# Last phase of a two-layer kernel: input norm statistics moved to ScalarE, and one scale and reciprocal for both hidden tiles

## The chip, the cores and the metric

The kernel runs on one core of one Trainium2 chip. The time is that of the device in microseconds (us) for one execution. An execution was profiled by itself; its time stands beside its span, from the first to the last instruction. The engines are TensorE (PE; PEld is its weight load), VectorE (DVE), ScalarE (ACT), GpSimd (POOL) and SyncE (SP), which issues direct transfers. They run side by side, each through its own list of instructions in order, and wait for one another on semaphores.

## The reference

Two layers work on x of shape 16 x 256 x 128 in float32. Each has a token-mixing part and a feed-forward part, and each part adds to x what it computes from a layer norm of x:

```
x = x + L0_attn(layernorm(x))     # gated linear attention
x = x + L0_ffn(layernorm(x))      # shared expert and one of 8 routed experts
x = x + L1_attn(layernorm(x))     # input projection, conv of 4 taps, state scan, gate, output projection
x = x + L1_ffn(layernorm(x))      # FP4-quantised gate, up and down projection
layernorm(x) = (x - mean(x)) / sqrt(var(x) + 1e-5)    # over the last 128 values
```

L1_attn takes 256 inner values: `xs = silu(conv(x w_in))`, a scan `h = 0.9 h + 0.1 (xs w_B)`, and `y = (h w_C) * silu(z)`, projected by `w_out`. L1_ffn quantises its input and its hidden vector in blocks of 16: `scale = max(|block|) / 6`, at least 1e-12; each value over its scale goes to the nearest point of an FP4 grid and is multiplied by the scale again. The hidden vector has 352 values, 22 blocks.

## The kernel before

Three phases follow one another: attention and shared expert of layer 0 (`phase_ab`), the routed experts (`phase_c`), and the whole of layer 1 (`phase_d`), which is the only one that the change touches. `phase_d` starts at 372 us and fills the rest of the span.

A token lies on one of the 128 partitions, so the 256 tokens of a sequence are a pair of tiles of 128 x 128. `phase_d` is a software pipeline over the 16 sequences. Each engine runs `body(j)` for j from -4 to 15; `run_skewed` writes out -4 to 0 and 11 to 15, and puts 1 to 10 in a hardware loop, two to a pass, in which semaphore values and tile addresses come from registers. POOL's list is written out in full. Within one body five sequences are worked on at different stages: `e = j + 4` has its input norm, `a = j + 3` its projection, convolution (on PE, as shifted products), Silu and scan, `b = j + 2` the gate, the output projection, the second norm and the input quantiser, `c = j + 1` the gate and up products and the hidden quantiser, and `d = j` the rescale, the down product and the store.

The order within a body is written by hand, and every hand-off is a semaphore. An engine that waits holds back all that stands behind.

- The input norm of e: DVE runs two bn_stats (`norm_stats`, L1835) early in the body and two bn_aggr (`norm_aggr`, L1842) later, which give mean and variance of both tiles in `mv`. POOL makes the factor and the offset in four small operations (`norm_sums`, L1691 to L1698) behind those of the second norm, and then issues the two gathers that add the routed experts' rows to x for the sequence two bodies on (L1676). ACT applies the norm at the end of the body (`xn`, L1800). PE transposes `xn` in the next body (L2016).
- The second norm of b has the same form (`stats4`, `mv4`, `shift4`, `xn4`, L1771).
- ACT's order: copies of `xqT` and `xnT`, the two Silus of the feed-forward (L1758), copies of `hqT`, `xn4` of b, `xs` of a (L1778), the hidden quantiser's two magnitudes (L1302), `zs` of a (L1788), the input quantiser's magnitude, `us` (L1795), `xn` of e.
- PE's order: `ps_Y` of b from the scan (L2002), transposes of `xq` and `xn`, the output projection from `yz` (L2023), gate and up products of c, transposes of `hq`, convolution products into `ps_A` and gate products into `ps_Z` (L206 to L208), the state matmuls from `xs` (L2076), the down product (L2089).
- The hidden quantiser of c (`Fp4`, `hidden_step`) on DVE, for two tiles t: block maxima (step 0, L1314), scale (1, L1316), reciprocal (2, L1318), division (3, L1320), and two rounding steps (4 and 5, L1323 and L1324), the last in the next body; then POOL multiplies by the scale (L1298). Steps 0 to 3 are issued step by step, tile 0 and then tile 1, so that scale and reciprocal are four operations on 128 x 22.

At the start of the phase the last groups of the shared expert still run (`late_up`, `late_silu`, `late_hidden`, `late_down`) and stand ahead of, or between, the first bodies on PE, ACT and DVE.

Of the kernel before, what the change touches and what calls it, by code (L numbers as in the profile page):

```python
# [28 lines left out]
P = 128  # L29
# [1249 lines left out]
class Fp4:  # L1279
# [296 lines left out]
def phase_d(nc, io, g, out):  # L1576
# [6 lines left out]
    with ExitStack() as ctx:  # L1583
# [13 lines left out]
        stats = sb("stats", [P, 2, 6])  # L1597
        mv = sb("mv", [P, 2, 2])
# [23 lines left out]
        fp4_h = [Fp4(nc, sb, f"fh{t}", F) for t in range(2)]  # L1622
# [6 lines left out]
        def halved(a):  # L1629
# [3 lines left out]
        (s_st, s_ln, s_eps, s_pow, s_nb, s_xn, s_xp, s_xT, s_p, s_z, s_zs, s_silu, s_u, s_us, s_scan, s_yp, s_yz, s_o,  # L1633
         s_x4) = (sem(n) for n in (
             "s_st", "s_ln", "s_eps", "s_pow", "s_nb", "s_xn", "s_xp", "s_xT", "s_p", "s_z", "s_zs", "s_silu", "s_u",
             "s_us", "s_scan", "s_yp", "s_yz", "s_o", "s_x4"))
        (s_st4, s_ln4, s_eps4, s_pow4, s_nb4, s_xn4, s_qz, s_mag, s_low, s_lowq, s_qx, s_magx, s_xq, s_xqp, s_xqT, s_gu, s_sg, s_h, s_qh, s_hq, s_hp, s_hT,
         s_f, s_x5, s_out) = (sem(n) for n in (
             "s_st4", "s_ln4", "s_eps4", "s_pow4", "s_nb4", "s_xn4", "s_qz", "s_mag", "s_low", "s_lowq", "s_qx", "s_magx", "s_xq", "s_xqp", "s_xqT", "s_gu", "s_sg",
# [31 lines left out]
        @blk_.gpsimd  # L1671
        def _(pool):
            def gather(n):

                for t in (2 * n, 2 * n + 1):
                    nc.gpsimd.indirect_dma_start(  # L1676
                        out=x[:, t, :], out_offset=None, in_=g["yg_dram"][:, :],
                        in_offset=bass.IndirectOffsetOnAxis(ap=g["pos"][:, t:t + 1], axis=0),
                        compute_op=ALU.add).then_inc(s_gather[n % 2], 16)

            nc.gpsimd.memset(hs[:, :], 0.0).then_inc(s_wz, 1)
            nc.gpsimd.memset(decay[:, :], 0.9).then_inc(s_wz, 1)
# [4 lines left out]
            def norm_sums(mean_var, to, nb, s_l, s_x, s_e, s_p, s_done, j):  # L1687
                wait(pool, s_l, j)
                wait(pool, s_x, j, ago=1)
                apart(pool)  # L1690
                nc.gpsimd.tensor_scalar(to, mean_var[:, :, 1], 1.0, EPS_LN, ALU.mult, ALU.add).then_inc(s_e, 1)  # L1691
                wait(pool, s_e, j)
                nc.gpsimd.tensor_tensor(to, to, halves[:, 0:2], ALU.pow).then_inc(s_p, 1)
                wait(pool, s_p, j, per=2)
                nc.gpsimd.tensor_tensor(nb, mean_var[:, :, 0], to, ALU.mult).then_inc(s_p, 1)
                wait(pool, s_p, j, n=2, per=2)
                apart(pool)
                nc.gpsimd.tensor_scalar(nb, nb, -1.0, None, ALU.mult).then_inc(s_done, 1)  # L1698

            def body(j):  # L1700
                b, d, e = j + 2, j, j + 4
                if live(d):
                    for t in range(2):
                        wait(pool, s_qh, d, n=t + 1, per=2)
                        wait(pool, s_hp, d, n=t + 1, per=2, ago=1)
                        fp4_h[t].rescale(nc.gpsimd, hq[:, t, :]).then_inc(s_hq, 1)
                if live(b):
                    norm_sums(mv4[:, :, :], rstd4[:, :], shift4[:, :], s_ln4, s_xn4, s_eps4, s_pow4, s_nb4, b)
                if live(e):
                    norm_sums(mv[:, :, :], rstd[:, :], shift[:, :], s_ln, s_xn, s_eps, s_pow, s_nb, e)  # L1710
                if live(e + 2):
                    if (e.off + 2) % 2 == 0 and e.off + 2 >= 2 * EARLY:
                        pool.wait_ge(s_ladd, (e.off + 2 - 2 * EARLY) // 2 + 1)
                    gather(e.off + 2)

            for j in range(FIRST, LAST + 1):
                body(Seq(j))

        @blk_.scalar
        def _(act):  # L1720
# [20 lines left out]

            def body(j):
# [24 lines left out]
                if live(b):  # L1767
                    wait(act, s_nb4, b)
# [11 lines left out]
                if live(c):  # L1780
                    for t in range(2):
                        act.wait_ge(s_qz, c.lin(10, 7 + t))
                        wait(act, s_qh, c, n=t + 1, per=2, ago=1)
                        fp4_h[t].magnitude().then_inc(s_mag, 1)
# [11 lines left out]
                if live(e):  # L1796
                    wait(act, s_nb, e)
                    wait(act, s_xp, e, ago=1)
                    for t in range(2):
# [9 lines left out]
        def _(dve):  # L1809
# [19 lines left out]
            PER = 10  # L1829
# [15 lines left out]
            def hidden_step(c, n, t):  # L1845

                if n == 0:
                    wait(dve, s_h, c, n=t + 1, per=2)
                elif n == 4:
                    wait(dve, s_mag, c, n=t + 1, per=2)  # L1850
                else:
                    if n == 1:
                        wait(dve, s_hq, c, n=t + 1, per=2, ago=1)
                    dve.wait_ge(s_qz, c.lin(PER, 2 * n - 1 + t))
                fp4_h[t].step(n, hid[:, t, :]).then_inc(s_qz if n < 5 else s_qh, 1)

# [15 lines left out]
            def body(j):  # L1872
# [36 lines left out]
                if live(c):  # L1909
                    for t in range(2):  # L1910
                        wait(dve, s_sg, c, n=t + 1, per=2)
                        nc.vector.tensor_tensor(hid[:, t, :], silu[:, t, :], (ps_U, ps_Z)[t][:, 0:F], ALU.mult).then_inc(s_h, 1)
                        if t == 0 and live(b):
                            wait(dve, s_nb4, b, ago=1)
                            norm_aggr(b, stats4, mv4, s_st4, s_ln4)
                    for n in range(4):
                        for t in range(2):
                            hidden_step(c, n, t)
                elif live(b):
                    wait(dve, s_nb4, b, ago=1)  # L1920
# [199 lines left out]
```

## Time and profile before

| | |
|---|---|
| time, median of 3 runs | 615.96 us (612.94 to 616.2) |
| the profiled execution's own time | 608.28 us |
| its span, instructions | 606.5 us, 15160 |
| TensorE's mean granted clock | 0.973 |
| busy over the span: PE, PEld | 541.1 us (89%), 443.1 us (73%) |
| busy over the span: DVE, ACT, POOL | 447.7 us (74%), 316.7 us (52%), 342.8 us (57%) |
| gathers into x on POOL (L1676), 32 | 57.3 us, 1791 ns each |
| rescale on POOL (L1298), 32 | 27.9 us, 890 ns each |

"Busy" adds up the durations of an engine's instructions; waits and semaphore work are not in it. Instructions of one engine may overlap by some 0.1 us, the next starting while the last one ends, so what an instruction costs in a row is the distance from its start to the next one's. A matmul's end is modelled. A granted clock of 1.00 is TensorE's 2.4 GHz, 0.50 its 1.2 GHz.

### The profile page before, as it was taken

How to read it: one execution, taken by the hardware profiler on the slowest of the kernel's cores; microseconds unless marked ns; L12 is line 12 of the kernel's file. 1: busy time of each engine (PE TensorE's matmuls, PEld its weight loads, DVE VectorE, ACT ScalarE, POOL GpSimd, SP SyncE). 2: the span in 40 equal slices, each digit the busy share in tenths (PEclk: the TensorE clock that was granted, in tenths of full speed). 3: DMA queues.
4: the chain of work that ended last, by engine and by line, in shares of the span. 5: the costliest groups of instructions: out<-in, count | busy, mean ns of one | idle time of the engine just before them, and what ended most of it. 6: DMA issues, size and time to landing. Idle time of an engine off the chain costs nothing. (4 is left out here: it accounts for less than half of the span.)

```text
span 606.5 us, 15160 instructions
## 1 busy us (share of the span) xinstructions
PE 541.1 (89%) x4517; PEld 443.1 (73%) x4518; DVE 447.7 (74%) x1179; ACT 316.7 (52%) x899; POOL 342.8 (57%) x514
## 2 busy tenths in 40 slices
PE   1799999999999898987999997998999999999955
PEld 1557667767767577777989996787778877887854
DVE  2689999899988449933575342468999989999873
ACT  2355676666666554304655652435545565456432
POOL 5468777777777522256764103746757777673231
PEclk9999999999999999996999998999999999999976
DMA  7000100100110164015222301200111111110000
GB/s 211 22 19 29 46 28 27 49 28 26 39 39 26 56 185 119 1 33 137 68 51 56 52 27 30 28 10 9 23 32 18 17 17 22 30 17 9 10 19 17
DMA packets 35193, 25.55 MB, mean 42 GB/s; under 512 B 4752, under 2 KB 31568, under 8 KB 35152
## 3 DMA queue, kind: packets, MB, share of 16 engines
q1 hardware_dynamic: 29264, 20.32, 11.4%
q0 software_dynamic: 5888, 4.72, 5.0%
q8 instruction: 20, 0.33, 0.2%
q14 instruction: 21, 0.17, 0.1%
HBM read 14.09 MB, written 6.75 MB: 34 GB/s over the span
## 5 line engine op out<-in xcount | busy, mean ns | idle before, releaser
L1135 PE MATMUL a_ps_a<-a_qx,a_kt 32*128 32x512 f32 x512 | 69.1, 628 | 1.0 <-DMA a_qx<-a_qs 1.0
L1676 POOL DMA_INDIRECT x<-yg_dram,pos x32 | 57.3, 1791 | 10.8 <-issue 10.8
L1298 POOL TENSOR_TENSOR d_hq<-d_fh_v,d_fh_scale 128x352 f32<-128x352 f32 x32 | 27.9, 890 | 57.1 <-DVE d_fh_v L1324 57.1
L440 POOL TENSOR_SCALAR_AFFINE_SELECT a_at<-a_at 128x512 f32<-128x512 f32 x80 | 50.7, 653 | 14.4 <-ACT a_at L521 14.4
L198 POOL DMA_INDIRECT rows<-xn_dram,slot_token x40 | 40.0, 999 | 32.0 <-ACT c_rows L1447 19.0
L521 ACT ACTIVATE a_at<-a_ps_a 128x512 f32<-128x512 f32 x80 | 44.5, 599 | 11.5 <-PE a_ps_a L1135 9.9
L1490 DVE TENSOR_TENSOR c_hid<-c_act,c_ps 128x352 f32<-128x352 f32 x39 | 20.2, 519 | 38.5 <-ACT c_act L1433 38.5
L1135 PEld LDWEIGHTS a_ps_a<-a_qx,a_kt 32*128 32x128 f32 x512 | 31.7, 188 | 16.9 <-issue 16.3
L206 PE MATMUL d_ps_A<-d_xnT,wmix 128*128 128x256 f32 x128 | 37.1, 290 | 0.6 <-ACT d_silu L1758 0.6
L704 DVE TENSOR_TENSOR a_at<-a_ps_a,mask 128x512 f32<-128x512 f32 x48 | 32.8, 685 | 6.3 <-PE a_ps_a L1135 5.2
L1433 ACT ACTIVATE c_act<-c_ps 128x352 f32<-128x352 f32 x39 | 18.1, 465 | 36.7 <-PE c_ps L208 36.7
L207 PE MATMUL d_ps_A<-d_xnT,wmix 128*128 128x256 f32 x128 | 36.1, 282 | 0.0
L208 PE MATMUL d_ps_A<-d_xnT,wmix 128*128 128x256 f32 x128 | 36.0, 282 | 0.0
L1059 PE MATMUL a_ps_o<-a_at,a_vpad 128*32 128x128 f32 x1024 | 34.6, 276 | 0.0
L466 POOL TENSOR_TENSOR a_kt<-a_e,a_rope 128x512 f32<-128x512 f32 x16 | 20.4, 1277 | 21.5 <-ACT a_e L557 21.5
L1546 PE MATMUL c_ps_y<-w,c_hidT 128*128 (+1 forms) x234 | 30.0, 277 | 1.6 <-ACT c_hidT L1459 1.6
L206 PE MATMUL c_ps<-w13p,c_xT 128*128 x78 | 29.8, 382 | 1.5 <-issue 0.5
L2089 PEld LDWEIGHTS d_ps_G<-d_wd,d_hqT 128*128 128x128 f32 (+1 forms) x192 | 23.8, 199 | 8.7 <-issue 5.5
L1546 PEld LDWEIGHTS c_ps_y<-w,c_hidT 128*128 128x128 f32 (+1 forms) x234 | 27.6, 191 | 2.3 <-issue 2.2
L789 DVE RECIPROCAL a_c<-a_c 128x128 f32<-128x128 f32 x32 | 29.1, 939 | 0.0
L2089 PE MATMUL d_ps_G<-d_wd,d_hqT 128*128 128x128 f32 (+1 forms) x192 | 27.0, 292 | 2.0 <-ACT d_hqT L1766 2.0
L1059 PEld LDWEIGHTS a_ps_o<-a_at,a_vpad 128*32 128x32 f32 x1024 | 26.0, 109 | 3.4 <-issue 3.0
(336 smaller groups left out, 1758.6 us busy)
## 6 DMA issues: line engine op xcount, KB each, us to landing
a_qx<-a_qs SPq DMA_DIRECT2D x64, 64.0 KB, 1.9
a_at<-in_L_ffn_w_eDF_dram SPq DMA_DIRECT2D x16, 176.0 KB, 3.2
yg_dram<-c_y SPq DMA_DIRECT2D x19, 128.0 KB, 1.8
xn_dram<-a_xn2s SPq DMA_DIRECT2D x16, 128.0 KB, 1.9
out_dram<-x SPq DMA_DIRECT2D x16, 128.0 KB, 1.9
w<-in_L_ffn_w_eFD_dram SPq DMA_DIRECT2D x2, 512.0 KB, 5.1
x<-in_L_attn_x_dram SPq DMA_DIRECT2D x1, 768.0 KB, 5.4
rows<-xn_dram,slot_token POOLq DMA_INDIRECT x40, 2.7
```

Of the source, the lines that this page charges most:

```text
L198: nc.gpsimd.indirect_dma_start(out=g["rows"][:, k % 4, t, :], out_offset=None, in_=g["xn2_dram"][:, :], in_offset=bass.IndirectOffsetOnAxi ...
L206: nc.tensor.matmul(to, left(0), right(0), start=start, stop=False)
L207: nc.tensor.matmul(to, left(0), right(1), start=False, stop=False)
L208: return nc.tensor.matmul(to, left(1), right(0), start=False, stop=stop)
L440: nc.gpsimd.affine_select(at[:, t, r, :, :], at[:, t, r, :, :], pattern=[[0, 4], [1, P]], compare_op=ALU.is_ge, fill=0.0, base=0, channel_ ...
L521: nc.scalar.activation(at[:, t, r, :, :], ps_a[:, r, :, :], ACT.Copy).then_inc(s_copied, 1)
L704: nc.vector.tensor_tensor(at[:, t, r, :, :], ps_a[:, r, :, :], mask[:, 0:1, :].to_broadcast([P, 4, P]), ALU.mult).then_inc(s_masked, 1)
L1059: last = nc.tensor.matmul(ps_o[32 * r:32 * r + 32, tile(t)], vpad[:, b.par, t, c0:c0 + 32], at[:, t, r, h, :], start=(t == 0 and h == 0), ...
L1135: last = nc.tensor.matmul(ps_a[:, r, :, :], kt[rows, b.par, c_, tile(t)], qx[rows, b.par, :, c_, tile(t)], start=(c_ == 0), stop=(c_ == 1))
L1546: last = nc.tensor.matmul(ps_y[:, t, :], hidT[0:fn, f.par, t, n, :], w2[0:fn, e_out[t], n, :], start=(n == 0), stop=(n == 2))
L1676: nc.gpsimd.indirect_dma_start(out=x[:, t, :], out_offset=None, in_=g["yg_dram"][:, :], in_offset=bass.IndirectOffsetOnAxis(ap=g["pos"][:, ...
L2089: last = nc.tensor.matmul(ps_G[:, P * t:P * t + P], hqT[0:fn, t, f, :], wd[0:fn, f, :], start=(f == 0), stop=(f == 2))
```

## The change

The four DVE instructions of the input norm go. In their place ACT makes two passes over each tile of e: `sums`, a Copy that also adds up the row (`total`), placed ahead of the Silus; and, after POOL has made `less` = -total / 128, `squares`, a Square with bias `less` that adds up the squared deviations (`square`), placed between `xn4` of b and `xs` of a. What the two passes write elementwise goes to a tile that nobody reads. POOL makes `less` right after its rescale of the hidden tiles and, behind the second norm's operations, factor and offset from `square`: three operations where there were four. `rstd` and `shift` mean what they meant.

The hidden quantisers of the two tiles share one tensor each for maxima, scales and reciprocals. Maxima and division stay one instruction for each tile; scale and reciprocal become one instruction each on 128 x 44 (`hidden_scales`), which waits for the maxima of both tiles. Semaphores for the two norms are counted in one (`s_nb`, `s_nb4`) instead of three; that changes no order.

```diff
@@ class Fp4
-    def __init__(self, nc, sb, name, width):
+    def __init__(self, nc, sb, name, width, small=None):
-        self.amax, self.scale, self.inv = (sb(f"{name}_{n}", [P, self.blocks]) for n in ("amax", "scale", "inv"))
+        self.amax, self.scale, self.inv = small or [sb(f"{name}_{n}", [P, self.blocks]) for n in ("amax", "scale", "inv")]
@@ phase_d, gpsimd, body
                         fp4_h[t].rescale(nc.gpsimd, hq[:, t, :]).then_inc(s_hq, 1)
+                if live(e):
+                    wait(pool, s_st, e)
+                    wait(pool, s_ln, e, ago=1)
+                    apart(pool)
+                    nc.gpsimd.tensor_scalar(less[:, :], total[:, :], -1.0 / D, None, ALU.mult).then_inc(s_nb, 1)
                 if live(b):
...
                 if live(e):
-                    norm_sums(mv[:, :, :], rstd[:, :], shift[:, :], s_ln, s_xn, s_eps, s_pow, s_nb, e)
+                    wait(pool, s_ln, e)
+                    wait(pool, s_xn, e, ago=1)
+                    apart(pool)
+                    nc.gpsimd.tensor_scalar(rstd[:, :], square[:, :], 1.0 / D, EPS_LN, ALU.mult, ALU.add).then_inc(s_nb, 1)
+                    wait(pool, s_nb, e, n=2, per=4)
+                    nc.gpsimd.tensor_tensor(rstd[:, :], rstd[:, :], halves[:, 0:2], ALU.pow).then_inc(s_nb, 1)
+                    wait(pool, s_nb, e, n=3, per=4)
+                    nc.gpsimd.tensor_tensor(shift[:, :], less[:, :], rstd[:, :], ALU.mult).then_inc(s_nb, 1)
@@ phase_d, scalar
+            def sums(e):
+                act.wait_ge(s_gather[e.par], e.half(32, 32))
+                wait(act, s_nb, e, n=1, per=4, ago=1)
+                apart(act)
+                for t in range(2):
+                    last = nc.scalar.activation(unused[:, 0, t, :], x[:, e.lin(2, t), :], ACT.Copy, accum_out=total[:, t:t + 1])
+                last.then_inc(s_st, 1)
+
+            def squares(e):
+                wait(act, s_nb, e, n=1, per=4)
+                wait(act, s_nb, e, n=2, per=4, ago=1)
+                apart(act)
+                for t in range(2):
+                    last = nc.scalar.activation(unused[:, 1, t, :], x[:, e.lin(2, t), :], ACT.Square, bias=less[:, t:t + 1],
+                                                accum_out=square[:, t:t + 1])
+                last.then_inc(s_ln, 1)
...
                     late_silu(4)
+                if live(e):
+                    sums(e)
                 if live(c):
...
                     last.then_inc(s_xn4, 1)
+                if live(e):
+                    squares(e)
                 if live(a):
@@ phase_d, vector
-            PER = 10
+            PER = 8
+            amax, scale, inv = (a[:, :, :].rearrange("p t b -> p (t b)") for a in both)
...
+            def hidden_scales(c):
+
+                wait(dve, s_hq, c, n=2, per=2, ago=1)
+                dve.wait_ge(s_qz, c.lin(PER, 2))
+                nc.vector.tensor_scalar(scale, amax, -1.0 / 6.0, -1e-12, ALU.mult, ALU.min).then_inc(s_qz, 1)
+                dve.wait_ge(s_qz, c.lin(PER, 3))
+                nc.vector.reciprocal(inv, scale).then_inc(s_qz, 1)
...
-                if live(e):
-                    dve.wait_ge(s_gather[e.par], e.half(32, 32))
-                    norm_stats(e, stats, s_st, s_ln)
...
-                if live(e):
-                    wait(dve, s_nb, e, ago=1)
-                    norm_aggr(e, stats, mv, s_st, s_ln)
...
-                    for n in range(4):
-                        for t in range(2):
-                            hidden_step(c, n, t)
+                    for t in range(2):
+                        hidden_step(c, 0, t)
+                    hidden_scales(c)
+                    for t in range(2):
+                        hidden_step(c, 3, t)
```

## Rows read from the trace of the kernel before

**Rows 1.** Windows: stretch, length, each engine's busy us (instructions), PE clock, DMA share, GB/s
```profile
374.00:375.60 1.60, 1.60 (x5) 1.21 (x5) 0.00 (x0) 0.00 (x0) 1.29 (x2) 0.50 0.00 0
480.00:492.00 12.00, 11.36 (x80) 9.64 (x79) 11.09 (x36) 6.88 (x19) 8.78 (x12) 1.00 0.13 21
```

**Rows 2.** Chain that ended last: start us, us, what; the gate product of four iterations
```profile
465.12 0.70 DVE d_yz L1878
...
489.82 0.70 DVE d_yz L1878
...
563.70 0.70 DVE d_yz L1878
...
575.98 0.70 DVE d_yz L1878
```

**Rows 3.** Timeline, ACT, one loop iteration: start, us, operation [idle before, releaser]
```profile
480.49 0.47 ACT L1758 ACTIVATE d_silu<-d_ps_G 128x352 f32<-128x352 f32 x1 [2.11 <-PE d_ps_U L208]
...
483.77 0.88 ACT L1771 ACTIVATE d_xn<-x,d_shift,d_rstd 128x128 f32 x2 [0.93 <-POOL d_shift L1698]
485.15 0.84 ACT L1778 ACTIVATE d_xs<-d_ps_A,cb 128x256 f32<-128x256 f32 x2 [0.49 <-PE d_ps_A L208]
...
487.43 0.36 ACT L1795 ACTIVATE d_us<-d_ps_M 16x256 f32<-16x256 f32 x1
```

**Rows 4.** Timeline, DVE, the same loop iteration
```profile
478.92 0.48 DVE L1835 BATCH_NORM_STATS2 d_stats<-x 128x6 f32 x2
...
480.50 0.24 DVE L1842 BATCH_NORM_AGGREGATE d_mv<-d_stats 128x2 f32<-128x6 f32 x2
...
482.31 0.94 DVE L1314 TENSOR_REDUCE d_fh_amax<-d_hid 128x22 f32<-128x352 f32 x2
483.17 0.30 DVE L1316 TENSOR_SCALAR d_fh_scale<-d_fh_amax 128x22 f32<-128x22 f32 x2
...
483.74 0.93 DVE L1320 SCALAR_TENSOR_TENSOR d_fh_v<-d_hid,d_fh_inv 128x352 f32<-128x352 f32 x2
```

**Rows 5.** Timeline, ACT, iteration 12, which has no pair to normalise
```profile
566.60 0.47 ACT L1758 ACTIVATE d_silu<-d_ps_G 128x352 f32<-128x352 f32 x1 [2.03 <-PE d_ps_U L208]
...
569.64 0.88 ACT L1771 ACTIVATE d_xn<-x,d_shift,d_rstd 128x128 f32<-128x128 f32 x2 [0.73 <-POOL d_shift L1698]
```

**Rows 6.** Groups by form, ACT, before the phase: count, busy us, mean ns, idle before
```profile
L557 ACT ACTIVATE a_e<-a_ps_c,a_nm 128x128 f32<-128x128 f32 x32 | 9.9, 362 | 0.0
...
L583 ACT ACTIVATE a_vpad<-a_ps_m 128x128 f32<-128x128 f32 x32 | 7.2, 277 | 1.7 <-PE a_ps_o L1059 0.9
...
L560 ACT ACTIVATE a_de<-a_nm 128x1 f32<-128x1 f32 x16 | 3.3, 205 | 0.0
...
L512 ACT ACT_TABLE_LOAD x1 | 1.3, 1283 | 0.8 <-PEq L2109 0.8
L651 ACT ACT_TABLE_LOAD x1 | 1.3, 1283 | 0.0
```

**Rows 7.** Timeline, POOL, one loop iteration
```profile
479.91 1.74 POOL L1298 TENSOR_TENSOR d_hq<-d_fh_v,d_fh_scale 128x352 f32<-128x352 f32 x2 [2.02 <-DVE d_fh_v L1324]
...
488.31 2.03 POOL L1676 DMA_INDIRECT x<-yg_dram,pos  x1 [0.30 <-issue]
```

**Rows 8.** Timelines of ACT, POOL and PE, start of the phase
```profile
380.83 0.60 ACT L1727 ACTIVATE d_late_act<-d_ps_A 128x512 f32<-128x512 f32 x1 [0.78 <-PE d_ps_Z L208]
382.37 0.88 ACT L1800 ACTIVATE d_xn<-x,d_shift,d_rstd 128x128 f32<-128x128 f32 x2 [0.94 <-POOL d_shift L1698]
...
399.04 0.82 ACT L1778 ACTIVATE d_xs<-d_ps_A,cb 128x256 f32<-128x256 f32 x2
...
380.65 0.19 POOL L1691 TENSOR_SCALAR d_rstd<-d_mv 128x2 f32<-128x2 f32 x1
...
383.60 0.38 PE L2016 MATMUL d_ps_H<-mask,d_xn 128*128 128x128 f32 x2
...
399.91 0.39 PE L2076 MATMUL d_ps_M<-d_xs,wb 128*16 128x256 f32 x1
```

More of the change, by code:

```diff
@@ L1596, in phase_d @@
         wd = sb("wd", [P, 3, D])
-        stats = sb("stats", [P, 2, 6])
-        mv = sb("mv", [P, 2, 2])
+        total = sb("total", [P, 2])
+        less = sb("less", [P, 2])
+        square = sb("square", [P, 2])
+        unused = sb("unused", [P, 2, 2, D])
         rstd = sb("rstd", [P, 2])
@@ L1621, in phase_d @@
         fp4_x = Fp4(nc, sb, "fx", 2 * D)
-        fp4_h = [Fp4(nc, sb, f"fh{t}", F) for t in range(2)]
+        both = [sb(f"fh_{n}", [P, 2, F // QB]) for n in ("amax", "scale", "inv")]
+        fp4_h = [Fp4(nc, sb, f"fh{t}", F, [a[:, t, :] for a in both]) for t in range(2)]
         ps_T, ps_Y, ps_G, ps_U, ps_A, ps_Z, ps_H, ps_M = (bank("ps_" + n) for n in "TYGUAZHM")
@@ L1685, in _, with norm_sums @@
                 gather(n)
-            def norm_sums(mean_var, to, nb, s_l, s_x, s_e, s_p, s_done, j):
+            def norm_sums(mean_var, to, nb, s_l, s_x, s_n, j):
                 wait(pool, s_l, j)
@@ L1690, in norm_sums @@
                 apart(pool)
[L1691 to L1696, printed above, removed]
+                nc.gpsimd.tensor_scalar(to, mean_var[:, :, 1], 1.0, EPS_LN, ALU.mult, ALU.add).then_inc(s_n, 1)
+                wait(pool, s_n, j, n=1, per=4)
+                nc.gpsimd.tensor_tensor(to, to, halves[:, 0:2], ALU.pow).then_inc(s_n, 1)
+                wait(pool, s_n, j, n=2, per=4)
+                nc.gpsimd.tensor_tensor(nb, mean_var[:, :, 0], to, ALU.mult).then_inc(s_n, 1)
+                wait(pool, s_n, j, n=3, per=4)
                 apart(pool)
-                nc.gpsimd.tensor_scalar(nb, nb, -1.0, None, ALU.mult).then_inc(s_done, 1)
+                nc.gpsimd.tensor_scalar(nb, nb, -1.0, None, ALU.mult).then_inc(s_n, 1)
             def body(j):
@@ L1706, in body @@
                         fp4_h[t].rescale(nc.gpsimd, hq[:, t, :]).then_inc(s_hq, 1)
+                if live(e):
[3 more added lines that the diff above has]
+                    nc.gpsimd.tensor_scalar(less[:, :], total[:, :], -1.0 / D, None, ALU.mult).then_inc(s_nb, 1)
                 if live(b):
-                    norm_sums(mv4[:, :, :], rstd4[:, :], shift4[:, :], s_ln4, s_xn4, s_eps4, s_pow4, s_nb4, b)
+                    norm_sums(mv4[:, :, :], rstd4[:, :], shift4[:, :], s_ln4, s_xn4, s_nb4, b)
                 if live(e):
-                    norm_sums(mv[:, :, :], rstd[:, :], shift[:, :], s_ln, s_xn, s_eps, s_pow, s_nb, e)
+                    wait(pool, s_ln, e)
[6 more added lines that the diff above has]
+                    nc.gpsimd.tensor_tensor(shift[:, :], less[:, :], rstd[:, :], ALU.mult).then_inc(s_nb, 1)
                 if live(e + 2):
@@ L1767, in body @@
                 if live(b):
-                    wait(act, s_nb4, b)
+                    wait(act, s_nb4, b, n=4, per=4)
                     wait(act, s_xq, b, ago=1)
@@ L1781, in body @@
                     for t in range(2):
-                        act.wait_ge(s_qz, c.lin(10, 7 + t))
+                        act.wait_ge(s_qz, c.lin(8, 5 + t))
                         wait(act, s_qh, c, n=t + 1, per=2, ago=1)
@@ L1796, in body @@
                 if live(e):
-                    wait(act, s_nb, e)
+                    wait(act, s_nb, e, n=4, per=4)
                     wait(act, s_xp, e, ago=1)
+                    apart(act)
                     for t in range(2):
@@ L1848, in hidden_step @@
                     wait(dve, s_h, c, n=t + 1, per=2)
+                elif n == 3:
+                    dve.wait_ge(s_qz, c.lin(PER, 4))
                 elif n == 4:
@@ L1851, in hidden_step @@
                 else:
-                    if n == 1:
-                        wait(dve, s_hq, c, n=t + 1, per=2, ago=1)
-                    dve.wait_ge(s_qz, c.lin(PER, 2 * n - 1 + t))
+                    dve.wait_ge(s_qz, c.lin(PER, 7 + t))
                 fp4_h[t].step(n, hid[:, t, :]).then_inc(s_qz if n < 5 else s_qh, 1)
+            def hidden_scales(c):
[4 more added lines that the diff above has]
+                nc.vector.reciprocal(inv, scale).then_inc(s_qz, 1)
             def input_step(b, n):
@@ L1913, in body @@
                         if t == 0 and live(b):
-                            wait(dve, s_nb4, b, ago=1)
+                            wait(dve, s_nb4, b, n=4, per=4, ago=1)
                             norm_aggr(b, stats4, mv4, s_st4, s_ln4)
-                    for n in range(4):
-                        for t in range(2):
-                            hidden_step(c, n, t)
+                    for t in range(2):
[3 more added lines that the diff above has]
+                        hidden_step(c, 3, t)
                 elif live(b):
-                    wait(dve, s_nb4, b, ago=1)
+                    wait(dve, s_nb4, b, n=4, per=4, ago=1)
                     norm_aggr(b, stats4, mv4, s_st4, s_ln4)
```

8 lines of the change are left out of this document (4 added, 4 removed).

## Prediction

> **What bounds the kernel now.** The change touches only the last phase, so I read its stretch of the windows table first. In the steady loop VectorE (DVE) has 11.09 us of instruction time in 12, ScalarE (ACT) 6.88, GpSimd (POOL) 8.78, and TensorE (PE) 11.36 at full clock [rows 1]. By shares alone DVE looks like an engine to relieve and ACT like one with room. The chain of waits says otherwise [rows 2]. It runs through PE and leaves it only for short hand-offs: the output gate `d_yz` on DVE, and `d_xs`, the Silu on ACT that the state matmuls wait for. Two loop iterations take 489.82 - 465.12 = 24.70 us, 12.35 each.
>
> The trace holds a natural experiment. From iteration 12 on there is no pair left to normalise, so DVE runs no input statistics, and POOL and ACT nothing of that norm. That iteration takes 575.98 - 563.70 = 12.28 us [rows 2]. Taking the statistics off DVE, and more with them, is therefore worth about 0.07 us an iteration. This is why I don't read 92% on DVE as a bound.
>
> Third, ACT's own order [rows 3]. Between the copy of `xnT` and the first Silu it idles 2.11 us. It then idles 0.93 us for POOL's `shift4` and 0.49 us for PE's `ps_A` ahead of `d_xs`. The `xn4` pair starts at 483.77 with 0.40 us from one to the next (0.88 for two of 0.48), so ACT is free at 484.57 and has 0.58 us until `d_xs` at 485.15. From there it runs without a gap, through two magnitudes, `zs`, `fx_k` and `us`; `us` feeds the scan and the scan feeds PE. A delay of `d_xs` is thus passed on whole.
>
> **What the change does, part by part.** *DVE statistics out.* Two bn_stats and two bn_aggr go in each of 16 iterations. The statistics pair holds DVE 0.39 us (478.92 to the next instruction) and the aggregation pair 0.22 us (480.50 to the next) [rows 4], 0.6 us together. What is late next: the product `d_hid` waits for the first Silu, which waits for PE. The hidden rescale on POOL starts 0.4 us earlier, but the projection of the next sequence waits for the second Silu all the same. I take the gain at 0.07 us by [rows 2]; the bounds are 0 and 0.6.
>
> *Sums on ACT (two Copy).* They stand ahead of the Silu in the 2.11 us gap. A 128x128 Copy of immediates took 277 ns [rows 6] and ACT instructions overlap by about 0.1 us (two `d_xs` of 0.47 in 0.84 [rows 3]), so 0.18 us each, plus whatever it costs to write the accumulator. No row shows that cost. Bounds: nothing, or a whole small instruction of 205 ns (128x1 [rows 6]) that starts only when its activation is done. I take 0.10 us each: a 128x1 instruction less the overlap. The pair costs 0.56, at most 1.0 us, hidden by the gap.
>
> The Trainium skill (VectorE: DVE Perf Modes, § Two Vector instructions with no wait between them) says that an accumulator output makes two instructions, the operation and a read of the accumulator. It says so of VectorE; the trace of before has no such operation on either engine. If ACT does likewise, that speaks for my middle value and against the lower bound.
>
> *Squares on ACT.* These stand between the `xn4` pair and `d_xs`, where room is short. A 128x128 activation with a pointer bias took 362 ns (the Exp of phase one [rows 6]), 0.26 us in a row. With 0.10 for the read the pair is 0.72 us, plus some 0.1 us for the nop and waits with register values in the loop, 0.82. The room is 0.58 us, and it grows: without statistics the step from first Silu to `xn4` is 569.64 - 566.60 = 3.04 us, against 483.77 - 480.49 = 3.28 [rows 3, 5]. Half of that difference I count to DVE, half to the unrolled code: room 0.70. So `d_xs` slips by 0.12, and as cover is gone it costs 0.12; with the gain of 0.07 the loop loses 0.05. The wake-up from POOL may cost a little too; I take 0.1 us an iteration, 1.0 us for ten. Lower bound: squares hidden, -0.7 us. Upper: reads in full behind their activations, 2 x (0.36 + 0.20) + 0.1 = 1.22, less 0.70 is 0.52, less 0.07 is 0.45, so 4.5 us. Iterations -1, 0 and 11 are unrolled and have about 0.8 us of room: nothing.
>
> *Iteration -2.* Here `d_xs` follows the `xn4` pair with no gap (399.04), and PE takes up the state matmuls at 399.91, just as it ends [rows 8]. The squares of the third pair now lie in front: 0.8 us less 0.2 that DVE gives back, 0.6 us (0.3 to 1.0).
>
> *Start.* The first norm becomes a relay of ACT, POOL, ACT, POOL, ACT. Before: first small POOL operation at 380.65, `xn` at 382.37, and PE transposes at 383.60, right behind its own work [rows 8]. After: ACT must first leave the late Silu (380.83 + 0.60), sums until 382.05, POOL's new `less` until 382.45, squares until 383.3. POOL then needs some 0.2 to wake and 1.3 of the former 1.7 us (its negation goes), so 384.8; `xn` 0.88 until 385.7. PE's transposes slip from 383.60 to 385.75, 2.15 us, and nothing in PE's order can pass them. Bounds 1.6 (reads free) and 2.9.
>
> *POOL.* One operation is added and one removed, but the norm of pair e now starts after the squares, some 1.6 us later than the DVE aggregate allowed, and the two gathers stand behind it. They ended at 488.31 + 2.03 = 490.34; POOL idled 2.02 us before the rescale [rows 7]. About 1.3 us of that is used up, 0.6 is left: no cost, at most 0.2 us an iteration. The gathers' data are used two iterations on.
>
> *Scale and reciprocal once.* From the start of the first of four small operations to the first `fh_v` it is 483.74 - 483.17 = 0.57 us [rows 4]. Halving would save 0.28. But the maxima end at 482.31 + 0.94 = 483.25, after the old first scale had already started; the merged one must wait for both tiles, then the reciprocal for it over twice the elements. I take no change in the loop, where ACT's queue ends last anyway, and +0.1 us over two passes of the tail (-0.5 to +0.4).
>
> **Sum.** 2.15 + 1.0 + 0.6 + 0.1 = 3.9 us. A stall of 2.15 us on PE may also drop its clock. At the start of the phase it was granted 0.50, the 1.2 GHz level, for some 3 us after a pause [rows 1]; again that would be 1.5 us, one chance in five, 0.3 us. Forecast +4.2 us. The profiled execution took 608.28 us (span 606.5 and 1.78 around it), so 612.5; the median of the runs shown is 615.96, 1.3% above it. The ratio 1.0069 gives 620.2 us.
>
> **Rivals.** (a) *It hides.* Squares fit in the loop and only the start and iteration -2 pay: +2.2 us, 618.2. For it: the room of 0.70 is near the price. Against: ACT has no slack behind `d_xs`. 26%. (b) *The reads drain.* Upper bounds of start, loop and iteration -2, 2.9 + 4.5 + 1.0 = 8.4, with the clock 9.9: 626. For it: a read of the accumulator can't come before the last element. 18%. (c) *DVE bounds.* If DVE's 0.6 us comes off 11 iterations at the hand-off `d_yz`, -6.6 + 2.15 is -4.4 us, 611.5. It decides if DVE was still busy when `ps_Y` was done. For it: 11.09 of 12. Against: the 12.28 us of the iteration without statistics. 6%. (d) *POOL bounds,* gathers delaying the rescale: +0.5 us in ten iterations on top of the forecast, 625. 2%. (e) *Tables.* Square might need another table than Silu. Phase one loads a table in 1283 ns once, and loads another for Silu later [rows 6]; two loads in each of 16 iterations are 41 us, 661. 2%.
>
> The Trainium skill (ScalarE: Activation LUTs, § Table sets: the hidden batching unit) says tables come in named sets and that cheap functions such as copy, identity and abs are in every set; Square is not named in that sentence. The trace agrees for those three, which alternate with Silu in the last phase; of Square beside Silu no row tells.
>
> **Numbers.** Forecast 46%, own range 619.0 to 623. Less than 0.5% (3.1 us) can't be told from no change here. Slower by more: forecast, (b), (d), (e), 0.46 + 0.18 + 0.02 + 0.02, less 0.02 for a forecast that falls short of the line: 0.66. Faster: (c), 0.06. The same: 0.28. Range 615.0 to 627.0: it takes in (a), (b) and (d), leaves out (c), (e) and ends of both sides.
>
> **What would show it.** `d_xs` in the loop starts straight after the second square with no idle time for PE's `ps_A`; PE waits for `d_xs` longer than before; the period is 12.35 to 12.5 us. First transposes of the normalised pair on PE at 385.5 to 386.2. Reads of the accumulator as rows of 0.2 us or none. DVE idles more before `d_hid`, and its share falls by some 3 points without the period following. I am wrong if the period falls below 12.2 us, if PE's start slips by under 1.5 us, or if table loads appear.

## The result, and the profile after

The changed kernel takes 619.16 us (median of 7 runs, 617.24 to 619.88), the kernel before 613.84 us (7 runs, 610.97 to 616.2). The ratio is 1.0082, with a 95% interval of 1.006 to 1.0104: slower, by 5.3 us. The forecast was a ratio of 1.0069 and 620.2 us.

Engines' busy time of the changed kernel's profiled execution (share of its span of 617.6 us, count of instructions):

```profile
PE 544.5 (88%) x4517; PEld 445.3 (72%) x4518; DVE 442.0 (72%) x1083; ACT 336.3 (54%) x1027; POOL 336.7 (55%) x514
```

The kernel before has 447.7 us in 1179 instructions on DVE and 316.7 us in 899 on ACT. DVE lost 96 instructions: 64 of statistics (four in each of 16 iterations), and 32 more because two scales and two reciprocals became one of each. ACT gained 128, not 64. The timeline of one loop iteration on ACT says why, and it is the main view of this case (start us, us, operation, idle before it and what ended it):

```profile
478.12 0.47 ACT L1792 ACTIVATE d_silu<-d_ps_G 128x352 f32<-128x352 f32 x1 [1.45 <-PE d_ps_U L208]
...
481.26 0.88 ACT L1805 ACTIVATE d_xn<-x,d_shift,d_rstd 128x128 f32 x2 [0.79 <-POOL d_shift L1701]
482.04 0.39 ACT L1770 ACTIVATE d_unused<-x,d_less 128x128 f32 x1
482.34 0.19 ACT L1770 ACTIVATION_READ_ACCUMULATOR d_unused<-x,d_less 128x1 f32 x1
482.43 0.39 ACT L1770 ACTIVATE d_unused<-x,d_less 128x128 f32 x1
482.72 0.19 ACT L1770 ACTIVATION_READ_ACCUMULATOR d_unused<-x,d_less 128x1 f32 x1
482.82 0.81 ACT L1814 ACTIVATE d_xs<-d_ps_A,cb 128x256 f32<-128x256 f32 x2
```

Each activation with an accumulator output is two instructions. The read has a row of 0.19 us and lengthens the row of work by 0.09 to 0.10 us (482.34 to 482.43). The pair of squares takes ACT's queue from 482.04 to 482.82, 0.78 us. Before, `d_xs` had 0.49 us of idle time for PE's `ps_A` in front of it [rows 3]; now there is none, so `d_xs` goes when the second read is done and no longer when its data are there. The copies ahead of the Silu end inside the gap for PE: it was 2.11 us [rows 3] and is still 1.45, so they delay nothing there.

The same stretch of the loop in the windows view (length, busy us of each engine with its instructions, PE's granted clock, DMA share, GB/s), to compare with [rows 1]:

```profile
480.00:492.00 12.00, 11.20 (x79) 9.60 (x78) 10.58 (x30) 7.63 (x27) 7.58 (x12) 1.00 0.14 22
```

DVE fell from 11.09 to 10.58 us and PE is no busier (11.20 us, 11.36 before). The gate products of the chain, against [rows 2]:

```profile
475.21 0.70 DVE d_yz L1924
...
500.00 0.70 DVE d_yz L1924
...
574.27 0.70 DVE d_yz L1924
586.56 0.70 DVE d_yz L1924
```

Two loop iterations take 24.79 us (before 24.70), and iteration 12, without a pair to normalise, 12.29 (before 12.28).

At the start of the phase the chain of waits shows the relay (start us, us, what; "issue" and queue pieces left out):

```profile
386.54 0.69 ACT d_unused L1762 x4
...
387.40 0.25 POOL d_less L1714
...
387.73 0.89 ACT d_unused L1770 x4
...
388.77 0.20 POOL d_rstd L1721
...
389.05 0.74 POOL d_rstd L1723
...
389.86 0.21 POOL d_shift L1725
...
390.15 0.89 ACT d_xn L1837 x2
...
391.17 0.58 PE d_ps_H L2058 x2
```

From the first sum to the transposes this relay takes 4.6 us, with five hand-offs from one engine to another. Before, PE took up the transposes right behind its own work [rows 8]. Now its timeline has a hole:

```profile
391.17 0.58 PE L2058 MATMUL d_ps_H<-mask,d_xn 128*128 128x128 f32 x2 [2.12 <-ACT d_xn L1837]
```

And behind the hole its clock is down, in windows of one microsecond:

```profile
390.17:391.17 1.00, 0.00 (x0) 0.03 (x1) 0.00 (x0) 0.86 (x2) 0.95 (x1) 1.00 0.00 0
391.17:392.17 1.00, 1.00 (x4) 0.90 (x5) 0.00 (x0) 0.38 (x1) 0.69 (x1) 0.55 0.00 0
392.17:393.17 1.00, 1.00 (x4) 0.80 (x3) 0.42 (x1) 0.00 (x0) 1.00 (x1) 0.50 0.53 65
393.17:394.17 1.00, 1.00 (x4) 0.72 (x3) 0.00 (x0) 0.00 (x0) 0.58 (x1) 0.50 0.10 17
```

0.50 is the level of 1.2 GHz; PE ends four matmuls in each such microsecond, and six to eight where the clock stays at 1.00 (after_again, below).

**The last phase as intervals.** All comparisons below use this table. It is made from the timelines: the phase starts with POOL's `memset` of `d_hs`; "start" runs from there to PE's first transposes of `d_xn`; "to gate" on to the first gate product `d_yz` on DVE (iteration -3); an iteration is the time from one `d_yz` to the next, named by the one it ends with; "loop" is the mean of iterations 1 to 10; "tail" runs from the last `d_yz` to the end of the span. Iterations -1 and 0 together are 24.7 in every kernel but the two that the text names; 12 is 12.28 or 12.29 in all.

| kernel (us) | start | to gate | it. -2 | loop | it. 11 | tail | phase |
|---|---|---|---|---|---|---|---|
| before | 10.95 | 9.51 | 10.27 | 12.33 | 12.29 | 30.52 | 233.85 |
| after | 13.44 | 11.10 | 11.04 | 12.38 | 12.45 | 31.04 | 239.87 |
| after, profiled again | 13.49 | 9.53 | 11.02 | 12.37 | 12.45 | 30.96 | 238.15 |
| stats_only | 13.49 | 11.06 | 11.03 | 12.37 | 12.49 | 30.45 | 239.24 |
| quant_only | 11.13 | 9.51 | 10.27 | 12.36 | 12.28 | 30.74 | 234.56 |
| pe_filler | 13.20 | 9.55 | 11.02 | 12.37 | 12.44 | 31.04 | 237.95 |
| squares_early | 13.52 | 9.52 | 10.25 | 12.30 | 12.28 | 31.10 | 236.70 |
| first_dve | 11.07 | 9.50 | 11.03 | 12.38 | 12.46 | 31.11 | 235.92 |
| squares_twice | 12.70 | 11.18 | 11.80 | 13.15 | 13.21 | 31.35 | 250.01 |
| best | 11.14 | 9.52 | 10.26 | 12.28 | 12.27 | 30.31 | 234.53 |
| before_filled | 11.12 | 9.51 | 10.27 | 12.33 | 12.29 | 26.94 | 230.43 |
| best_filled | 10.79 | 9.53 | 10.25 | 12.28 | 12.28 | 26.87 | 229.51 |

The phase of the profiled execution after is 6.0 us longer: start 2.5, clock behind it 1.6, iteration -2 0.8, loop 0.5, iteration 11 0.2, tail 0.5. The spans differ by 11.1 us. The other 5 us lie before the phase, in stages with the same code (the phase started at 377.73 instead of 372.65), and don't recur in the timed ratio, which is 5.3 us in all. A difference of two single profiled executions isn't the effect of the change; the stretch that the change touches is nearer to it.

### The profile page after: what moved, and what is told of

Same layout as the page of the kernel before. It is cut to its first block and busy times, and to the rows that moved or that the text cites. A ratio compares the mean times of both kernels' runs of the same rounds, so it can differ in the third digit from the quotient of the medians.

```text
span 617.6 us, 15179 instructions
## 1 busy us (share of the span) xinstructions
PE 544.5 (88%) x4517; PEld 445.3 (72%) x4518; DVE 442.0 (72%) x1083; ACT 336.3 (54%) x1027; POOL 336.7 (55%) x514
## 3 DMA queue, kind: packets, MB, share of 16 engines
q1 hardware_dynamic: 29264, 20.32, 11.1%
## 5 line engine op out<-in xcount | busy, mean ns | idle before, releaser
L1135 PE MATMUL a_ps_a<-a_qx,a_kt 32*128 32x512 f32 x512 | 70.6, 641 | 1.0 <-DMA a_qx<-a_qs 1.0
L1679 POOL DMA_INDIRECT x<-yg_dram,pos x32 | 52.9, 1653 | 7.7 <-issue 7.7
```

The costliest lines, as they stand in the source:

```text
L1135: last = nc.tensor.matmul(ps_a[:, r, :, :], kt[rows, b.par, c_, tile(t)], qx[rows, b.par, :, c_, tile(t)], start=(c_ == 0), stop=(c_ == 1))
L1679: nc.gpsimd.indirect_dma_start(out=x[:, t, :], out_offset=None, in_=g["yg_dram"][:, :], in_offset=bass.IndirectOffsetOnAxis(ap=g["pos"][:, ...
```

## The experiments

Each ratio is against the kernel before on the same chip. Three chips were used, on which the kernel before took 607.96, 612.38 and 612.65 us, so ratios are compared across them and times aren't.

**stats_only** is the changed kernel with the old order of the quantiser (and the semaphore counts that go with it):

```
-                    for t in range(2):
-                        hidden_step(c, 0, t)
-                    hidden_scales(c)
-                    for t in range(2):
-                        hidden_step(c, 3, t)
+                    for n in range(4):
+                        for t in range(2):
+                            hidden_step(c, n, t)
```

> The statistics of the input norm on ACT as in the changed kernel; the hidden quantiser as before (a scale and a reciprocal for each tile). Theory: nearly all of the loss is in the statistics. The tail from the last-but-two gate product to the end falls back from 31.0 to 30.5 us, and in the loop nothing changes (12.38 us an iteration). Against before +5.5 us in the last phase by its profile, +4.5 us (+0.7%) in the timed runs. Rival: the merged scale and reciprocal delay the hidden rescale in every iteration and carry the loop's 0.05 us; then the loop goes back to 12.33 us and the sum to +3.5 us.

613.7 us, ratio 1.007 (1.0046 to 1.0095). **quant_only** is the reverse: the kernel before with only `hidden_scales` put in.

> Only one scale and one reciprocal for both hidden tiles; statistics on DVE as before. Theory: from first maximum to first division DVE takes 1.66 us instead of 1.43 in each iteration; hidden in the loop, paid in two passes of the tail: +0.5 us (+0.1%), not to be told from no change. Rival: DVE is nearly full before the change (11.1 of 12 us), so the 0.23 us shows in each of 10 to 13 iterations: +2.5 to +3 us (+0.45%).

609.46 us, ratio 1.0019 (0.9996 to 1.0042). The statistics carry the slowdown; the two parts add up to 1.0089, which fits 1.0082 and 1.0088 (after_again). The table puts the second part in the tail: 30.52 to 30.74 with it alone, 31.04 to 30.45 when it is taken out of the changed kernel. The loop mean of quant_only, 12.36, comes from one iteration, the first, which took 12.56 us against 12.32 before; the others are within 0.03 of those before, and no run tells why that one was longer.

**pe_filler** adds to the changed kernel eight matmuls of 512 columns, whose results nobody reads, in the hole of 2.1 us:

```
+                if a.m is None and a.off == 0:
+                    pe.wait_ge(s_lh, 3)
+                    f0, fn = FT[1]
+                    for r in range(4):
+                        for m, to in enumerate((ps_Y, ps_M)):
+                            nc.tensor.matmul(to[0:fn, :], ws1[:, 0, m, f0:f0 + fn], late[:, 1, 0, :], start=True, stop=True)
                 if live(a):
                     wait(pe, s_xn, a)
```

> The changed kernel with eight matmuls of 512 columns (1.9 us at full clock) that nobody reads, put on PE ahead of the first transposes of the normalised pair, where it stands still for 2.1 us. Theory: the pause costs twice, 2.3 us as waiting and 1.6 us because the clock falls to 0.50 behind it. With work in the pause the clock stays at 1.00, the first transposes come as late as now (2.3 us late against before) and the first gate product comes 9.5 us after them instead of 11.1: 1.6 us less than the changed kernel, +3.4 us against before. Rival: the clock falls anyway, at a moment of its own, and the time is that of the changed kernel, +5 us, or more by what the filler delays.

611.69 us, ratio 1.0048 (1.0028 to 1.0067). The clock stayed up, the stretch to the gate went from 11.10 to 9.55. That profile alone doesn't show that the filling did it, for the clock can stay up without it, as the unedited kernel, profiled again, shows:

> The changed kernel once more, beside the others on one chip. Theory: +0.8% against before; in its profile the same intervals of the last phase within 0.1 us, except the 3 us behind the first pair's pause, where the clock may fall (first gate product 11.1 us after the first transposes) or not (9.5 us), as it did not in the kernel with the squares moved. Rival: whether it falls is fixed by the kernel's own order, and it falls again.

618.56 us, ratio 1.0088 (1.006 to 1.0116). The same hole of 2.13 us stood in the timeline of its PE, and the clock did not fall (first row the timeline, then windows of 1 us):

```profile
393.04 0.41 PE L2058 MATMUL d_ps_H<-mask,d_xn 128*128 128x128 f32 x2 [2.13 <-ACT d_xn L1837]
```

```profile
393.10:394.10 1.00, 1.00 (x6) 0.87 (x7) 0.20 (x1) 0.38 (x1) 0.70 (x2) 1.00 0.00 0
394.10:395.10 1.00, 1.00 (x8) 0.87 (x7) 0.23 (x1) 0.22 (x1) 1.00 (x1) 1.00 0.54 66
```

**squares_early** is the changed kernel with the squares ahead of the `xn4` pair, where ACT waits for POOL anyway:

```
+                if live(e):
+                    squares(e)
                 if live(b):
                     wait(act, s_nb4, b, n=4, per=4)
...
-                if live(e):
-                    squares(e)
```

> The changed kernel with the squares ahead of the second norm's application on ACT, where ACT waits 0.8 to 0.9 us for POOL in the loop and 4.3 us in iteration -2. Theory: the squares (0.78 us) cost because they stand between that application and the Silu of the projection. Moved, the Silu follows PE again; iteration -2 takes 10.3 us instead of 11.0, iteration 11 12.3 instead of 12.45, the loop 12.28 to 12.33 instead of 12.38: 1.5 to 2 us less than the changed kernel, +3.3 us against before (+0.5%). Rival (POOL): POOL's relay sets the loop, so that its place on ACT matters little; the loop stays at 12.38 and the gain is at most 0.8 us. Rival (ACT full): the squares now delay the application of the second norm and with it the input quantiser; the loop gets longer than 12.4 us.

611.42 us, ratio 1.004 (1.0021 to 1.0059). Its timeline of ACT:

```profile
484.63 0.20 ACT L1770 ACTIVATION_READ_ACCUMULATOR d_unused<-x,d_less 128x1 f32 x1
484.99 0.88 ACT L1807 ACTIVATE d_xn<-x,d_shift,d_rstd 128x128 f32 x2 [0.16 <-POOL d_shift L1701]
486.37 0.84 ACT L1814 ACTIVATE d_xs<-d_ps_A,cb 128x256 f32<-128x256 f32 x2 [0.50 <-PE d_ps_A L208]
```

The idle time ahead of `d_xs` is back (0.50, before it was 0.49), so that PE's `ps_A` and no longer ACT's queue sets its start. The loop went from 12.38 to 12.30, iteration -2 from 11.04 to 10.25, iteration 11 from 12.45 to 12.28. By the table that is 0.8 + 0.8 + 0.2 = 1.8 us given back by moving two lines; the whole phase is 1.5 us shorter than in after_again, the execution of the changed kernel whose clock stayed up too.

**squares_twice** doubles the suspect: `squares` makes another pair, into buffers of its own.

```
+                for t in range(2):
+                    nc.scalar.activation(unused[:, 2, t, :], x[:, e.lin(2, t), :], ACT.Square, bias=less[:, t:t + 1],
+                                         accum_out=spare[:, t:t + 1])
...
```

> The changed kernel with the squares done twice (the second pair of passes goes to tiles that nobody reads). Theory: ACT's queue between the second norm's application and the Silu of the projection is full, so 0.78 us more of it are paid whole in each iteration: loop 12.37 + 0.75 = 13.1 us, +7.5 us over ten iterations, iteration -2 another 0.8, the start 0.8, in all +9 to +11 us over the changed kernel. Rival (some slack is left): ACT's rows overlap and the loop pays less than 0.4 us an iteration. Rival (POOL): POOL's gathers, 0.78 us later, delay the hidden rescale, and the loop pays more than 0.9.

630.4 us, ratio 1.0294 (1.0268 to 1.0321). The loop went from 12.38 to 13.15, 0.77 an iteration, which is the length of the pair (0.78; 486.64 - 485.87 here too). The second pair is paid whole. The first cost 0.05 in sum, or 0.08 without DVE's relief (12.38 against 12.30 of squares_early): that is the difference between work on a full queue and work in a gap.

```profile
484.31 0.88 ACT L1809 ACTIVATE d_xn<-x,d_shift,d_rstd 128x128 f32 x2 [0.80 <-POOL d_shift L1702]
485.09 0.39 ACT L1771 ACTIVATE d_unused<-x,d_less 128x128 f32 x1
...
485.87 0.39 ACT L1774 ACTIVATE d_unused<-x,d_less 128x128 f32 x1
...
486.64 0.82 ACT L1818 ACTIVATE d_xs<-d_ps_A,cb 128x256 f32<-128x256 f32 x2
```

PE pays it: its weight load's wait for `d_xs` in the view of waits (us in all, times, longest) was 6.1 us in 15 waits before, 7.9 us in the changed kernel, and of squares_twice it reads

```profile
PEld d_ps_M L2122 <- ACT d_xs L1818: 18.6, 15, 1.7
```

Against after_again on the same chip the time rose by 11.8 us, a little more than the 9 to 11 expected. The expectation had left out iterations -1, 0 and 11, which took 2.1 us more (-1 and 0 together 26.0 us). The start is short, 12.70, since the clock at the opening of the phase didn't drop; the late Silu began 6.80 us into the phase, 8.32 in the changed kernel. PE's hole ahead of the transposes is longer by the second pair, and the clock behind it fell to 0.50:

```profile
389.79 0.66 PE L2062 MATMUL d_ps_H<-mask,d_xn 128*128 128x128 f32 x2 [2.88 <-ACT d_xn L1841]
```

**first_dve** is the changed kernel with the statistics of the very first pair on DVE, as before; ACT's sums and squares and POOL's `less` start with the second pair:

```
+                if j.m is None and j.off == -4:
+                    dve.wait_ge(s_gather[0], 32)
+                    norm_stats(e, stats0, s_st, s_ln)
+                    norm_aggr(e, stats0, mv0, s_st, s_ln)
...
```

> The changed kernel, but the very first pair takes its statistics on DVE (bn_stats and bn_aggr) as before; the other fifteen on ACT. Theory: two thirds of the loss in the last phase are the first pair's relay (2.3 us of waiting on PE and, where the clock falls behind it, 1.6 us more). The first transposes return to 11.0 us after the start of the phase, the first gate product to 9.5 us after them; iteration -2 stays at 11.0, the loop at 12.37, the tail at 31.0. In sum +2 us against before (+0.35%). Rival: the start is hidden behind the second pair's relay, which still goes through ACT, POOL, ACT and POOL; then at most 1 us comes back and it stays at +0.7%.

613.45 us, ratio 1.0021 (1.0002 to 1.0041). The start is 11.07 again, the hole on PE is gone, and the rest is as in the changed kernel.

**best** takes out each cost that was found: the old quantiser, `squares_early` and `first_dve` together.

> Three things at once: statistics on ACT for all but the first pair, the squares ahead of the second norm's application, and the hidden quantiser as before. Theory: each removes one part of the loss and nothing is left but the relief of DVE: start 11.0 and 9.5 us, loop 12.30 against 12.33, tail 30.5; 0.3 us less than before, not to be told from no change (-0.1% to +0.1%). Rival: DVE's 0.6 us an iteration were worth having once ACT doesn't stand in the way; then the loop falls towards 12.0 us and the time by 3 us (-0.5%).

612.54 us, ratio 0.9989 (0.9965 to 1.0013): no difference from the kernel before that can be told. Its loop is 12.28 against 12.33, so the whole worth of DVE's relief is 0.05 us an iteration, 0.5 us in all by the profiles. It comes in one of the two iterations of a pass only: they take 12.22 and 12.38 us by turns, before 12.31 and 12.38. Its profiled execution took 1.2 us more in iterations -1 and 0 (25.9 us); PE's timeline and a window show that its clock fell there, behind a pause that the kernel before has too:

```profile
419.79 0.62 PE L2049 MATMUL d_ps_Y<-d_hs,wc 128*128 128x256 f32 x1 [1.57 <-DVE d_hs L1980]
```

```profile
420.00:421.00 1.00, 1.00 (x3) 0.79 (x3) 0.47 (x2) 0.00 (x0) 0.00 (x0) 0.50 0.35 45
```

**Filled pauses.** The table pointed at something larger than the change. In the tail of the kernel before, PE stands still twice for long, and its clock is 0.50 behind each pause (first the timeline of PE, then windows of 2 us):

```profile
586.74 0.69 PE L2010 MATMUL d_ps_T<-mask,d_xq 128*128 128x128 f32 x2 [3.89 <-DVE d_xq L1298]
...
598.62 0.90 PE L2050 MATMUL d_ps_H<-mask,d_hq 128*128 128x128 f32 x3 [2.86 <-POOL d_hq L1298]
```

```profile
588.00:590.00 2.00, 1.64 (x6) 1.64 (x7) 1.17 (x3) 0.00 (x0) 1.18 (x2) 0.50 0.22 60
...
602.00:604.00 2.00, 1.83 (x9) 1.53 (x8) 0.14 (x1) 0.00 (x0) 0.00 (x0) 0.50 0.00 0
```

**before_filled** is the kernel before with unread matmuls in these two pauses and in the one of 1.57 us; **best_filled** has them on top of best:

```
+            def filler(to, sem_, count, times):
+                pe.wait_ge(sem_, count)
+                for _ in range(times):
+                    nc.tensor.matmul(to[:, :], ws1[:, 0, 0, 0:P], late[:, 1, 0, :], start=True, stop=True)
...
+                    filler(ps_T, s_lowq, 1, 6)
...
+                if j.m is None and j.off == 14:
+                    filler(ps_M, s_x4, B, 15)
...
+                if j.m is None and j.off == 15:
+                    filler(ps_M, s_x4, B, 13)
```

> The kernel before, with matmuls that nobody reads in three pauses of PE in the last phase: 6 ahead of the first gate matmuls of iteration 0 (pause of 1.57 us), 15 ahead of the last transposes of the quantised input (pause of 3.9 us) and 13 ahead of the last transposes of the hidden vector (3.3 us). Theory: the clock of PE falls to 0.50 behind such pauses and halves what comes after; filled, it stays at 1.00 to the end and the tail (last gate product to the end) falls from 30.5 to about 27 us: -3.5 us, -0.6% against before. Rival: the clock falls all the same, or the chain there is DVE's and ACT's and doesn't mind a slow PE; then less than 1 us.

> The kernel with the statistics on ACT for all but the first pair, the squares moved ahead of the second norm's application and the old hidden quantiser, with the same filling of PE's pauses. Theory: both parts add up: loop 12.28 us, tail 27 us, -3.5 us of filling and -0.5 us of DVE's relief, -0.65% against before. Rival: no difference from the filled kernel before can be told, since 0.05 us an iteration is all the relief brings.

Both took 609.08 us against 612.65: ratios 0.9948 (0.9925 to 0.9971) and 0.995 (0.9922 to 0.9978). By these ratios both are faster than the kernel before, and they can't be told apart: the further 0.5 us that best_filled was to bring, if it is there, is below what the runs resolve. (The 3.3 us named for the second pause of the tail are those of best; in the kernel before it is 2.86.) The tail went from 30.52 to 26.94 and from 30.31 to 26.87, with the clock at 1.00 until PE's last matmul (before_filled):

```profile
586.00:588.00 2.00, 2.00 (x11) 1.67 (x11) 1.90 (x7) 1.22 (x4) 0.00 (x0) 1.00 0.00 0
...
602.00:604.00 2.00, 1.60 (x12) 1.41 (x12) 0.28 (x1) 0.02 (x1) 0.00 (x0) 1.00 0.00 0
```

## Why the prediction was right, and where its terms were not

- **Direction and mechanism: right.** 4.2 us were forecast, of them 3.9 as waiting and 0.3 as one chance in five of a lower clock; the timed kernels differ by 5.3 us (0.0082 of 613.84 is 5.0), the phase by 4.3 in the execution without a fall of the clock and 6.0 in the one with it. Part of the closeness is luck: the loop was put too high by 0.5 us, the start, iterations -2 and 11 and the tail too low by 1.1 together. The 620.2 us stand on a median of 615.96 of three runs; seven gave 613.84.
- **The natural experiment: right in size, but not by its reasoning.** The 0.07 us between the loop and iteration 12 were read as the worth of the statistics. But iteration 12 stands in the unrolled code, and iteration 11 before it, unrolled too and with all its statistics, takes the same 12.29 us (from 551.41 to 563.70 [rows 2]; timeline of DVE, kernel before):

```profile
551.41 0.69 DVE L1878 TENSOR_TENSOR d_yz<-d_ps_Y,d_zs 128x512 f32<-128x512 f32 x1
...
552.72 0.48 DVE L1835 BATCH_NORM_STATS2 d_stats<-x 128x6 f32<-128x128 f32 x2
...
554.30 0.24 DVE L1842 BATCH_NORM_AGGREGATE d_mv<-d_stats 128x2 f32<-128x6 f32 x2
```

  There the absence of the statistics was worth nothing, and the 0.07 can't be read as their worth. That the relief in the loop came out at 0.03 to 0.05, near to it, is shown by squares_early and best alone. Against rival (c) iteration 11 speaks even more plainly than iteration 12.
- **Start, +2.15 (1.6 to 2.9): measured +2.5.** Counted from the start of the late Silu (386.05 after), the working put the end of the sums at +1.22, of the squares at +2.5, of POOL's part at +4.0 and PE's transposes at +4.9; the rows give 1.18, 2.57, 4.01 and 5.12. The rest is that the late Silu itself came 0.14 later in the phase. The hole on PE is 2.12 us. first_dve took the term away alone (11.07).
- **The read of the accumulator, 0.10 us in a row: right**, by the rows above. The rule of the Trainium skill (VectorE: DVE Perf Modes, § Two Vector instructions with no wait between them), that an accumulator output makes two instructions, is stated of VectorE; ScalarE's rows here agree with it.
- **Iteration -2, +0.6 (0.3 to 1.0): measured +0.77**, the whole pair. The 0.2 us that DVE was to give back there did not come; squares_early set it to nothing.
- **Loop, +1.0 (-0.7 to 4.5): measured +0.5.** `d_xs` follows the second read without a gap, as said. The pair took 0.78, not 0.82 (no 0.1 for waits in front of it could be seen), so the slip was mis-sized: 0.08 (12.38 against 12.30 of squares_early), not 0.12; nor did the wake-up from POOL, for which the 0.05 so reckoned had been raised to 0.1 an iteration, show a cost.
- **Iteration 11, nothing: measured +0.16**, and it goes with squares_early. Before, ACT idled 0.69 us ahead of `d_xs` there; in the changed kernel the `xn4` pair, which waits for POOL, also starts 0.21 us later than before (6.25 us after the gate product, not 6.04), and `d_xs` starts 0.20 later. What holds POOL up there no run shows. Iterations -1 and 0 had the room.
- **Tail, +0.1 (-0.5 to 0.4): measured +0.5**, the term that missed by most for its size and fell out of its bounds. Both reasons had been named and were under-priced. In the last of the two passes of the kernel before, the maxima start at 593.22, the scales 0.86 later, the reciprocals 0.27 after them, and the first `fh_v` 0.35 after those: 1.48 us. In the first pass of the changed kernel (in both kernels the passes are alike in this) the maxima start at 591.36 and `fh_v` at 593.09; the merged scale comes 1.04 later, as it waits for the second maximum, the reciprocal 0.22 after it, and `fh_v` 0.47 after that, as it waits for twice the elements: 1.73 us.

```profile
592.40 0.19 DVE L1899 TENSOR_SCALAR d_fh_scale<-d_fh_amax 128x44 f32<-128x44 f32 x1
592.62 0.43 DVE L1901 RECIPROCAL d_fh_inv<-d_fh_scale 128x44 f32<-128x44 f32 x1
```

  0.25 us in each of two passes would be the 0.5. But in quant_only, with the same rows, the tail grew by only 0.2, and kernels with the same tail differ by 0.2 (30.31 to 30.52 in best, stats_only and before), where PE's clock rises and falls at other moments. The 0.25 us in a pass is shown; that two of them make up the whole 0.5 isn't. Where pairs follow each other without a gap, merging saved instructions here and lengthened the path to the first result. In the loop it costs next to nothing, as forecast: 12.38 against stats_only's 12.37.
- **Clock, one chance in five of 1.5 us.** The size was right (1.6). The clock fell in two of the four profiles with an unfilled hole of 2.1 us (after and stats_only; not in after_again and squares_early), and in squares_twice behind 2.88 us. One in five looks low, but so few profiles don't settle it, and how often it falls over all timed runs no trace tells.
- **Rivals.** It hides (a): not quite; the loop pays 0.05 an iteration, and squares_early shows where. The reads drain (b): no, 0.10. DVE bounds (c): no; DVE lost 0.5 us in 12 and best shows what that is worth. POOL bounds (d): no; it still idles 1.19 us for `d_fh_v` ahead of its rescale:

```profile
489.63 1.74 POOL L1298 TENSOR_TENSOR d_hq<-d_fh_v,d_fh_scale 128x352 f32<-128x352 f32 x2 [1.19 <-DVE d_fh_v L1324]
```

 Tables (e): no; the changed kernel has the two table loads of the kernel before, both ahead of this phase, and none with Square beside Silu.

What stays open: squares_early and pe_filler were each timed some 0.4% better than the changed kernel, 2.5 us, where their profiles give back 1.8 and, against an execution with the fall, 1.6. The intervals allow both. How much of pe_filler's gain comes from the clock is thus not shown. Nor is it known what decides whether the clock falls behind a pause of 1.6 to 2.9 us, or why the stages ahead of the phase took 5 us longer in the profiled execution.

## What to carry to other kernels

A busy share of 92% on one engine is by itself no reason to move work off it: look first for an iteration in the trace that lacks this work, and compare it with one of the same code that has it. Here iterations 11 and 12 of the unrolled code differed by nothing, and in the loop the relief of 0.6 us was worth 0.05. Then read where in the other engine's order the moved work comes to stand: the pair of squares cost nothing that shows in the gap of 0.9 us ahead of `xn4`, 0.08 in one of 0.5 us ahead of `d_xs`, and its full 0.78 on a full queue. A chain that goes to and fro between two engines is paid in the first pass, where nothing overlaps it (here 2.5 us); first_dve, which leaves that pass on DVE, got it back.

## What the runs showed of the hardware

- After pauses of PE of 3.9 and 2.9 us in the tail its clock was 0.50 in the kernel before. Behind 2.1 us it fell in two of four profiles, behind 2.88 us in the one that had it (squares_twice), behind 1.57 us in one (best), where nine profiles with the same pause kept 1.00. At the opening of the phase all twelve profiles have a pause of 2.4 us; behind it the clock was 0.50 for some 3 us in ten and stayed at 1.00 in two (squares_twice and best_filled). The same pause can thus cost or not, from one profile to the next. With the tail's pauses and the one of 1.57 us filled by unread matmuls, PE's mean clock was 0.990 instead of 0.973 and the tail 3.6 us shorter, seven times what DVE's relief was worth.
- ACT's accumulator output: a second row of 0.19 us, 0.10 in a row. A 128x128 Square with pointer bias and its read take 0.39 us in a row, a Copy and its read 0.29.
